# A mixture-of-experts walk: the multiplier read at a computed address, a step list made by matmul, experts built two ahead, clearing on ScalarE

## The reference, cut to what matters

```python
def _L0_ffn_ref(x, weight, scale, expert_masks, router_w):
    logits = jnp.einsum('bsd,ed->bse', x, router_w)
    probs = jax.nn.softmax(logits, axis=-1)
    top1_w = jnp.max(probs, axis=-1)
    top1_idx = jnp.argmax(probs, axis=-1)
    w_q = jnp.clip(jnp.round(weight / THRESH), -1.0, 1.0)
    w_scaled = w_q * scale[:, None]
    def body(out, inputs):
        e_idx, mask_e = inputs
        y = jnp.einsum('bsi,oi->bso', x, w_scaled * mask_e)
        sel = (top1_idx == e_idx)[..., None]
        out = jnp.where(sel, y * top1_w[..., None], out)
        return (out, None)
```

## Time and profile before

| what | value |
|---|---|
| median of 3 runs | 1764.93 us (1764.42 to 1766.23) |
| the profiled execution | 1765.17 us, span 1763.0 us |
| PE, DVE, ACT, POOL busy | 84%, 77%, 52%, 39% of the span |
| expert stage in the span | about 505 to 704 us |
| first and last product | 564.8 and 686.0 us |

### The profile page before, as it was taken

The page is one execution under the profiler, slowest core; times in us unless marked ns, Lnnn a source line. Parts: engine busy times, 40 slices in busy tenths (PEclk is TensorE's granted clock), DMA queues, the critical chain, the costliest instruction groups (busy, mean ns, idle before and its releaser), DMA issues. The chain is left out here.

```text
span 1763.0 us, 20903 instructions
## 1 busy us (share of the span) xinstructions
PE 1483.3 (84%) x6523; PEld 612.0 (35%) x6523; DVE 1366.0 (77%) x2046; ACT 910.9 (52%) x1201; POOL 687.1 (39%) x473
## 2 busy tenths in 40 slices
PE   5888998886753875589898988898899889899997
PEld 1333433332231422333244324433433334343433
DVE  6989989999988852689877966896688588747553
ACT  4766676564431100347753766476557544645553
POOL 3999999999934427000010010001000133434332
PEclk8999999999986998779999999999999999999999
DMA  7455455455568652510001000100010400000000
GB/s 244 120 151 147 137 153 155 132 151 152 160 140 212 155 120 90 197 33 1 1 13 33 1 13 1 33 1 1 1 34 1 100 1 1 24 1 25 1 24 24
DMA packets 65210, 131.52 MB, mean 75 GB/s; under 512 B 11328, under 2 KB 11328, under 8 KB 64336
## 3 DMA queue, kind: packets, MB, share of 16 engines
q1 hardware_dynamic: 53056, 104.07, 20.7%
q0 software_dynamic: 7168, 25.17, 6.3%
q10 hardware_dynamic: 4880, 0.95, 0.3%
HBM read 134.11 MB, written 12.85 MB: 83 GB/s over the span
## 5 line engine op out<-in xcount | busy, mean ns | idle before, releaser
L370 POOL TENSOR_TENSOR ssm_dBu<-ssm_du,ssm_BC 128x1024 f32<-128x1024 f32 x128 | 304.9, 2389 | 16.6 <-DVE ssm_du L406 16.6
L265 PE MATMUL ssm_psY<-ssm_hC,ident 128*128 128x512 f32 x512 | 254.2, 624 | 40.6 <-POOL ssm_hC L377 20.7
L1527 DVE TENSOR_REDUCE att_next_mx<-att_next_ring 128x1 f32<-128x512 f32 x384 | 241.8, 683 | 32.7 <-PE att_next_ring L1258 31.0
L334 ACT ACTIVATE ssm_dA<-ssm_delta,ssm_negA 128x512 f32<-128x512 f32 x256 | 165.3, 682 | 165.5 <-DVE ssm_hC L426 164.1
L1412 ACT ACTIVATE att_Pr<-att_next_psT 128x1024 f32<-128x1024 f32 x192 | 186.2, 1023 | 81.2 <-PE att_next_psT L1282 80.5
L1650 POOL TENSOR_TENSOR mlp_both<-mlp_first,mlp_third 128x512 f32<-128x512 f32 x88 | 124.8, 1419 | 227.6 <-DVE mlp_first L1873 142.5
L1873 DVE SCALAR_TENSOR_TENSOR mlp_first<-mlp_psQ,mlp_s_gu,mlp_first 128x512 f32<-128x512 f32 x176 | 131.6, 749 | 102.6 <-ACT mlp_first L1763 88.7
L1543 POOL TENSOR_TENSOR X<-X,late_bout 128x512 f32<-128x512 f32 x12 | 15.9, 1354 | 498.4 <-POOLq L65 498.4
L471 DVE TENSOR_TENSOR_SCAN ssm_dA<-ssm_dA,ssm_dBu 128x512 f32<-128x512 f32 x148 | 178.3, 1217 | 18.2 <-ACT ssm_dA L334 14.2
L265 PEld LDWEIGHTS ssm_psY<-ssm_hC,ident 128*128 128x128 f32 x512 | 94.7, 196 | 190.9 <-issue 86.1
L1700 PE MATMUL mlp_psD<-mlp_Wd,mlp_hT 128*128 128x512 f32 x352 | 157.4, 592 | 0.0
(11 more groups left out here) (314 smaller groups left out, 2485.0 us busy)
## 6 DMA issues: line engine op xcount, KB each, us to landing
ssm_BC<-bc_rows SPq DMA_DIRECT2D x128, 512.0 KB, 4.8
moe_W<-in_masksT POOLq DMA_DIRECT2D x32, 512.0 KB, 8.0
late_words<-in_gate_upT SPq DMA_DIRECT2D x32, 176.0 KB, 3.8
X<-in_x SPq DMA_DIRECT2D x4, 1024.0 KB, 11.0
rows<-moe_XP SPq DMA_DIRECT2D x4, 1024.0 KB, 14.4
out_x<-X SPq DMA_DIRECT2D x4, 1024.0 KB, 4.3
mlp_Wd<-in_downT SPq DMA_DIRECT2D x8, 352.0 KB, 9.5
ssm_ctxP<-in_ctxT SPq DMA_DIRECT2D x4, 512.0 KB, 12.3
```

What stands on the lines that cost most here:

```text
L265: nc.tensor.matmul(psY[:, w, :], ident[:], hC[:, w, g % RC, :], start=False, stop=(n == DS - 1)).then_inc(summed, 1)
L334: nc.scalar.activation(dA[:, q % RA, :], delta[:, b % 2, e, :], ACT.Exp, scale=negA[:, e, n:n + 1]).then_inc(dA_done, 1)
L370: nc.gpsimd.tensor_tensor(dBu[:, g % RB], du[:, b % 2, hh * W:(hh + 1) * W, :], BC[:, g % RING, 0, :].unsqueeze(1).broadcast_to([P, W, S]) ...
L1527: nc.vector.tensor_reduce(mx[:, m % 3, qt, row_order(j)], bank(("score", i)), AX.X, ALU.max).then_inc(maxed, 1)
```

## The change

The multiplier of `accumulate` is no longer copied: the accumulate reads it as its scalar operand straight from `GO` at the step's address. The step list is made with one step a partition (a compare over 32 columns and a sum), put on a diagonal, and spread to all partitions by a matmul with ones on PE into `psE`, from where DVE copies `EI` and `SI` as one tile of 2 x 47. `build(0)` moves ahead of the rank tables, `build(1)` behind the step list, and every later build runs as `build(k + 2)` after `accumulate(k)`. The result tiles are cleared by ScalarE, each batch after its rows are stored, in place of GpSimd.

```diff
                 for t in range(XR):
                     fetch(t)
-                for t in range(XR):
-                    clear(t)
                 for t in range(TILES):
                     if t + XR < TILES:
                         pool.wait_ge(parts, t + 1)
                         fetch(t + XR)
-                        clear(t + XR)
...
-                act.wait_ge(tables, 3)
+                for b in range(B):
+                    act.wait_ge(stored[b], 16)
+                    for t in range(b * NT, (b + 1) * NT):
+                        nc.scalar.activation(XP[:, t, :], keep[:], ACT.Copy, scale=0.0).then_inc(zeroed, 1)
+                act.wait_ge(tables, 2)
...
-                    if k >= 2:
-                        dve.wait_ge(acc_done, k - 1)
-                    nc.vector.tensor_copy(g[:, k % 2:k % 2 + 1], GO[:].rearrange("p t e -> p (t e)")[:, bass.ds(k * E - e * (E - 1), 1)]).then_inc(g_done, 1)
                     y = XP[:, t, :]
-                    dve.wait_ge(g_done, k + 1)
+                    member = GO[:].rearrange("p t e -> p (t e)")[:, bass.ds(k * E - e * (E - 1), 1)]
                     dve.wait_ge(zeroed, min(k + 1, TILES))
                     dve.wait_ge(mm_done, k + 1)
                     if k >= 1:
                         dve.wait_ge(acc_done, k)
-                    nc.vector.scalar_tensor_tensor(out=y, in0=psO[:, k % SLOTS, :], scalar=g[:, k % 2:k % 2 + 1], in1=y,
+                    nc.vector.scalar_tensor_tensor(out=y, in0=psO[:, k % SLOTS, :], scalar=member, in1=y,
...
                 chain.mark(nc.vector.reciprocal(gate[:], den[:]))
+                build(0)
                 dve.wait_ge(ranked, 1)
...
-                chain.link(nc.vector.tensor_tensor(CMP, rk.unsqueeze(1).broadcast_to([P, STEPS, E]),
-                                                   iota[:, 0:STEPS].unsqueeze(2).broadcast_to([P, STEPS, E]), ALU.is_lt))
-                chain.link(nc.vector.tensor_reduce(Ef[:], CMP, AX.X, ALU.add))
-                chain.link(nc.vector.tensor_scalar(Sf[:], Ef[:], float(NW), float(NW), ALU.is_ge, ALU.mult))
-                nc.vector.tensor_copy(EI[:], Ef[:]).then_inc(tables, 1)
-                nc.vector.tensor_tensor(SI[:], Ef[:], Sf[:], ALU.subtract).then_inc(tables, 1)
-                dve.wait_ge(tables, 3)
-                for e in range(SPARE + 1):
-                    build(e)
+                chain.link(nc.vector.tensor_scalar(step_of[:], rk, token[:, 0:1], None, ALU.is_lt))
+                chain.link(nc.vector.tensor_reduce(at_step[:, 0:1], step_of[:], AX.X, ALU.add))
+                chain.mark(nc.vector.tensor_scalar(diag[:, 0, :], ident[:, 0:STEPS], at_step[:, 0:1], None, ALU.mult))
+                chain.link(nc.vector.tensor_scalar(at_step[:, 1:2], at_step[:, 0:1], float(NW), -float(NW), ALU.is_ge, ALU.mult))
+                chain.link(nc.vector.tensor_tensor(at_step[:, 1:2], at_step[:, 0:1], at_step[:, 1:2], ALU.add))
+                nc.vector.tensor_scalar(diag[:, 1, :], ident[:, 0:STEPS], at_step[:, 1:2], None, ALU.mult).then_inc(listed, 1)
+                build(1)
+                dve.wait_ge(listed, 2)
+                nc.vector.tensor_copy(ESI[:].rearrange("p w k -> p (w k)"), psE).then_inc(tables, 1)
+                dve.wait_ge(tables, 2)
                 low_part(0)
                 low_part(1)
                 for k in range(STEPS):
                     if k + 2 < TILES:
                         low_part(k + 2)
                     accumulate(k)
-                    if k + SPARE + 1 < NW:
-                        build(k + SPARE + 1)
-                    if NW <= k + 2 < E:
+                    if k + 2 < E:
                         build(k + 2)
...
-                pe.wait_ge(tables, 3)
+                pe.wait_ge(listed, 1)
+                nc.tensor.matmul(psE, ones[:], diag[:].rearrange("p w k -> p (w k)"), start=True, stop=True).then_inc(listed, 1)
+                pe.wait_ge(tables, 2)
                 turn_rows(0)
                 turn_rows(1)
```

More of the change, by code:

```diff
@@ L549, in stage_experts @@
         IDX = sb("IDX", [P, TILES], U32)
[L550 to L553, removed]
+        step_of = sb("step_of", [P, E])
+        at_step = sb("at_step", [P, 2])
+        diag = sb("diag", [P, 2, STEPS], F16)
+        ESI = sb("ESI", [P, 2, STEPS], I32)
+        EI, SI = ESI[:, 0], ESI[:, 1]
         GO = sb("GO", [P, TILES, E])
@@ L560, in stage_experts @@
         rstd = sb("rstd", [P, TILES, 1])
-        g = sb("g", [P, 2])
         psO = ps("psO", [P, SLOTS, D])
@@ L576, in stage_experts @@
         tern32 = spare[:, 6144:8192]
-        CMP = spare[:, 0:STEPS * E].rearrange("p (k e) -> p k e", e=E)
         ends = spare[:, 0:E * TILES].rearrange("p (e t) -> p e t", t=TILES)
@@ L589, in stage_experts @@
         psI = psO[:, 2, 0:TILES]
+        psE = psO[:, 3, 0:2 * STEPS]
         negs = W[:, NW - 1, :]
@@ L598, in stage_experts @@
             "cum", "ranked", "pos_done", "tables", "parts", "evac", "zeroed"))
-        W_done, mm_done, g_done, acc_done, scaled = (sem(n) for n in (
-            "W_done", "mm_done", "g_done", "acc_done", "scaled"))
+        W_done, mm_done, acc_done, scaled, listed = (sem(n) for n in (
+            "W_done", "mm_done", "acc_done", "scaled", "listed"))
         stored = [sem(f"stored{i}") for i in range(B)]
@@ L623, in load_mask @@
                     pool.dma_start(W[:, e % NW, :], masks[e]).then_inc(mask_in[e % NS], 16)
-                def clear(t):
-                    nc.gpsimd.memset(XP[:, t, :], 0.0).then_inc(zeroed, 1)
                 def fetch(t):
```

## The result

| | before | after |
|---|---|---|
| median, same chip | 1764.42 us (1763.92 to 1766.23, 5 runs) | 1774.65 us (1771.65 to 1777.58, 5 runs) |
| ratio after to before | | 1.0042, 95% interval 1.0024 to 1.0061 |
| profiled execution, span | 1765.17, 1763.0 us | 1774.65, 1772.8 us |

By the medians the change made the kernel slower by 10.2 us; 1774.65 was measured and 1773.0, 8.0 more than before, had been forecast. The ratio, 1.0042, which is taken from the runs of both kernels, puts the loss at 7.4 us, with an interval of 4.2 to 10.8. The direction is clear of noise; its size is known to some 3 us.

What follows compares the result with a forecast made beforehand. DVE was taken to bound the kernel at 2.79 us a step, PE close behind. First accumulate 566.8 + 42.4 + 20.6 = 629.8, 8.0 late; 1764.93 + 8.0 = 1773.0 us, range 1765.5 to 1778.

Steps and rivals of the forecast that it cites:

- The start: Start of the walk: four of six builds leave the front, so the first product comes 4.15 us sooner, at 560.6.
- The cover of build(0) and of the clears: Before the walk: build(0) fits DVE's 1.29 us wait, sixteen clears fit ScalarE's 24.12 us idle time; both cost nothing.
- the list's gain: Before the walk: step list ready at about 553.7, not 557.21; worth nothing, as PE waits for gathered rows until 558.07.
- The one slow small operation: Old step list: one 47-column operation took 2.27 us; taken as an exception, with the new small operations at about 0.2.
- The turn with row turns: Steps 0 to 13: product, row turns, high part, low part, accumulate, build, product; 7.06 us for two steps.
- x: Steps 0 to 13: time from the high part's end to the accumulate; taken as 1.25 us, bounds 0.63 and 1.36.
- The rule of the Trainium skill: Steps 0 to 13: a 600 ns register load would hide behind the low part; rival of +4.3, 1769.3, chance 0.13.
- The turn without row turns: Steps 12 to 20: product, accumulate, build, next product, with no rows left to turn; 5.15 us, 2.58 a step.
- The sum: Whole walk: start, six turns of 42.4 us and four of 20.6 put accumulate 20 at 629.8, 8.0 us later.
- the ring: Walk up to step 29: product k, accumulate k, build k+2, product k+2 wait in a closed circle; 3.53 us a step early.
- DVE as the bound: Walk, thirteen steps: builds two ahead are early enough, a step costs about 2.55 us; -5.8, 1759.1, chance 0.10.
- The clock rival: Walk, PE: waits lower TensorE's clock, about 4.1 us a step, 8 us more, 1781; chance 0.04.

Runs made afterwards that it cites:

- three ahead: The changed kernel with builds three ahead up to expert 20, build 2 joining the two in front: 1756.28 us, ratio 0.9939.
- low part last: The changed kernel with the low part of tile k+2 moved behind accumulate k and build k+2 on DVE: 1764.28 us, ratio 0.9977.
- direct alone: The kernel before with only the copy of the multiplier removed, the accumulate reading it at the computed address: 1764.35 us, ratio 0.9984.
- six ahead: The changed kernel with builds six ahead again up to expert 20, builds 2 to 5 before the first low part: 1759.38 us, ratio 0.9944.
- order alone: The kernel before with only the build order changed: builds 0 and 1 in front, then build k+2 after each accumulate: 1779.05 us, ratio 1.0071.
- Load first: The changed kernel with DVE's register read of the step's expert moved ahead of the wait for the high part: 1770.32 us, ratio 1.0012.
- copy back: The changed kernel with the copy of the multiplier into g put back: 1775.52 us, ratio 1.0041.
- GpSimd's clears: The changed kernel with the clears of the result tiles back on GpSimd: 1775.10 us, ratio 1.0040.

## Why the prediction was right, point by point

- **The start.** First product forecast at 560.6, measured 560.70; first accumulate 566.8 and 566.84. The cover of build(0) and of the clears holds. That the list's gain is worth nothing holds for the profiled execution, and in this it was lucky: the cover of the list is the gather, and when that lands depends on the execution. In three ahead, low part last and direct alone the table of rows (`IDX`) was written 4 us later than in the kernel before (552.7), the gather landed sooner behind it, and PE waited for the list, the old one in direct alone (first fence) and the new one in three ahead (second fence):

```profile
561.26 1.97 PE L874 MATMUL moe_psX<-ident,moe_XS 128*128 128x128 f32 x8 [9.11 <-DVE moe_SI L830]
```

```profile
557.68 1.97 PE L876 MATMUL moe_psX<-ident,moe_XS 128*128 128x128 f32 x8 [1.03 <-DVE moe_ESI L832]
```

With `IDX` at the same time the early list starts the walk 3.6 us sooner. This fits the ratios above, which give the kernels with the early list 1 to 4 us less than their walks; how often an execution is of this kind was not measured. It bears on four builds in front as well: the new list is done at 557.6 in three ahead, four builds from there would end near 562.3 (an estimate from the 4.63 us of six ahead), and the high part is there at 559.5.

- **The one slow small operation.** The prediction left the 2.27 us of L831 as an exception. It runs while GpSimd clears four result tiles, and ends 0.05 us behind them; in order alone and direct alone, where the clears also fall on it, it takes 2.27 and 2.26. With the new list no such operation meets the clears, not even when they are back on GpSimd (first clear at 555.96, list done at 555.31). The row of the kernel before:

```profile
554.87 1.93 POOL L626 MEMSET moe_XP<- 128x512 f32 x4
```

That the clears cause the 2.27 is not shown: no run takes them away from the old list.

- **The turn with row turns.** Forecast 7.06, measured 42.43 / 6 = 7.07. Its unknown, x, was taken as 1.25 and is 1.19. Load first takes 0.55 out of x and shortens the turn by 0.64; low part last takes out the row turns, the high part and the address work and leaves 5.80 where 5.7 had been worked out. That the turn is the sum of these terms is so shown within 0.1 us.
- **The rule of the Trainium skill** (DMA: Bandwidth & Descriptors, section Latency and other measured facts: about 600 ns for a register load) would have given x = 0.63 and 1769.3. The trace does not agree, neither for the load itself, which took 0.307 us at 590.1 and never under 0.299, nor for the whole address: 1.19, and 0.64 only when the load was moved ahead of the wait.
- **The turn without row turns.** Forecast 5.15, measured 21.33 / 4 = 5.33. The mis-sized term is product end to accumulate, 0.41 before and 0.49 after; the rest is spread over the turn. Together with the steps above: accumulate 20 forecast 8.0 us late, measured 8.8.
- **After step 20** nothing changes: 66.29 and 65.95 us for accumulates 20 to 46. This, and the sliding of GpSimd's end by 8.8, were as forecast.
- **The sum.** -4.2 at the start, +8.4 and +4.6 in the two parts of the ring, -0.3 after: +8.5 at the last accumulate, 8.8 at the last return, against the 8.0 of the forecast. 1.6 more in attention is the clock, which the sum did not contain; the span ends 9.8 later.
- **The rivals.** DVE as the bound needed a turn under 5.1 and did not come; it is what three ahead and six ahead show, at 32.24 and 31.65 us where 2.55 a step had been worked out (30.6). The clock rival (0.04) did not happen in the changed kernel's walk. The reason given against it, that no gap in the ring is near 4.76 us, was weak: in the neighbours the clock fell behind waits of 1.48 to 2.00 us, where the changed kernel's longest is 1.16. Its price of 8 us was too high as well, since no fall lasted for the whole ring. The Trainium skill's warning (TensorE: Matmul & The Clock Gate, section HAM oscillation — how this bites in real kernels) is borne out in its neighbours: in copy back, GpSimd's clears and order alone the clock stood at 0.76 to 0.81 over stretches of 7 to 11 us of the ring, with 0.50 to 0.52 in the lowest 2 us of each. It is a matter of 1 us or so for each fall (two each in copy back and order alone), not of the 10.3 us that the order costs in order alone or the 15.9 between the walks of the changed kernel and six ahead.

## What to carry to other kernels

Where an order is written out by hand, the distance by which an engine works ahead closes a ring of waits. Add up one turn, divide by the steps that it advances, and compare with each engine's own work; here 7.07 / 2 was above 2.8 and 7.07 / 3 was not. An idle engine in front of the loop is the place for work ahead: in six ahead the early list left DVE the time in which four more builds fit. In this trace a register read that follows a wait in program order began only after that wait (590.1), and moving it ahead gained 3.8 us in twelve steps: put the read first.

## What had not been expected of the hardware

- Address work behind a wait cost 1.19 us from release to accumulate with 0.47 us idle, though the low part's 0.60 lay in between; with the read ahead of the wait it was 0.64. The register load is only 0.31 of it.
- TensorE's clock is 2.4 GHz (granted 1.00) in most of the ring. Waits of 1.48 (GpSimd's clears), 1.66 and 2.00 (copy back), 1.98 and 1.60 us (order alone) were followed by stretches with a granted clock well under 1.00 (0.76 to 0.81 in the stretches shown above), partly at the lower level of 1.2 GHz; four waits of 1.54 to 1.73 us in copy back, five of 1.42 to 1.74 in GpSimd's clears, five of 1.26 to 1.50 in order alone and those of up to 1.16 in the changed kernel were not. What decides it stays open.
- The same group of eight matmuls in attention took 3.58 us in one execution and 1.99 in the other. The runs of one kernel spread by up to 11 us on another chip (1761.82 to 1773.01 for the kernel before), which is more than most effects here; the part of the walk that no kernel changed repeats within 0.5 us (20-46: 65.88 to 66.31).
